# Own key tile of causal attention in fewer columns: values and probabilities repacked, the doubled high halves copied by VectorE

## The reference

```python
# x: (2, 512, 512) float32; Wq, Wo: 512 <-> 32*128; Wk, Wv: 512 -> 8*128
q = (x @ Wq).reshape(B, S, 32, 128).transpose(0, 2, 1, 3)
k = (x @ Wk).reshape(B, S,  8, 128).transpose(0, 2, 1, 3)   # each repeated for 4 query heads
v = (x @ Wv).reshape(B, S,  8, 128).transpose(0, 2, 1, 3)
scores = q @ k^T * 128 ** -0.5, masked causally
out = softmax(scores) @ v
x = layernorm(x + out.reshape(B, S, 4096) @ Wo)
# then a router with sparsemax over 8 low-rank experts:
base = x @ W_base^T + b_base
w = sparsemax(x @ W_router^T + b_router)
x = layernorm(x + base + sum_e w_e * (x @ A_e) @ B_e)
```

## Time and profile before

| | |
|---|---|
| median of 3 runs | 675.08 us (674.37 to 675.57) |
| span of the profiled execution | 673.6 us |
| TensorE busy | 657.9 us, 98%, 3605 matmuls |
| TensorE weight loads | 340.6 us, 51% |
| VectorE busy | 531.2 us, 79% |
| ScalarE busy | 416.8 us, 62% |
| GpSimd busy | 259.1 us, 38% |
| DMA moved | 71.80 MB, queue of SyncE and ScalarE 48.4% of 16 engines |

### The profile page before, as it was taken

How to read it: one execution, slowest core, us unless ns; L and a number is a source line. 1 busy time by engine, 2 the same in 40 slices (tenths; PEclk the granted TensorE clock), 3 DMA queues, 4 the chain that set the end, 5 groups by cost and what they waited for, 6 DMA issues and landing times.

```text
span 673.6 us, 11403 instructions
## 1 busy us (share of the span) xinstructions
PE 657.9 (98%) x3605; PEld 340.6 (51%) x3605; DVE 531.2 (79%) x1728; ACT 416.8 (62%) x1081; POOL 259.1 (38%) x246
## 2 busy tenths in 40 slices
PE   7899999999999999999999999999999999999996
PEld 3455455455555555455555545455554545455553
DVE  3899778867897688867797688867788578789866
ACT  3796665666556765667566765667556667866331
POOL 1686870166013750166013650167003613352231
PEclk9999999999999999999999999999999999999999
DMA  9357375354914285244924285353835247252602
GB/s 300 139 125 158 74 176 110 65 78 84 239 37 94 49 187 110 54 89 78 231 52 93 48 177 114 49 101 69 201 54 100 49 79 173 56 103 46 111 18 93
DMA packets 200779, 71.80 MB, mean 107 GB/s; under 512 B 169744, under 2 KB 192784, under 8 KB 200720
## 3 DMA queue, kind: packets, MB, share of 16 engines
q1 hardware_dynamic: 199376, 70.04, 48.4%
q10 hardware_dynamic: 1344, 1.05, 0.6%
HBM read 27.02 MB, written 2.10 MB: 43 GB/s over the span
## 4 chain that ended last, share of the span: by engine, by line
PE 89%; DVE 5%; DMA 3%; ACT 1%; POOL 1%; issue 1%; SPq 0%; DVEq 0%; POOLq 0%
PE bank L1259 23%; PE bank L1210 21%; PE bank L1249 15%; PE bank L1234 12%; PE bank L1222 5%; PE bank L1190 4%; PE bank L1291 2%; PE bank L1203 2%; PE bank L1193 2%; DMA pT<-p 2%; DVE p L1065 1%; PE bank L1183 1%; DVE pr L1045 1%; DVE rowmax L946 1%; PE bank L1302 1%
## 5 line engine op out<-in xcount | busy, mean ns | idle before, releaser
L741 POOL TENSOR_SCALAR raw<-raw,scale_of 128x512 f32<-128x512 f32 (+1 forms) x75 | 120.6, 1608 | 315.3 <-ACT wk L807 189.1
L1045 DVE CUSTOM_DVE_ANT_0 pr<-bank,mask,back_of 128x32 f32<-128x32 f32 (+15 forms) x256 | 125.3, 496 | 58.4 <-PE bank L1234 57.6
L863 ACT ACTIVATE pr<-pr,mx 128x288 f32<-128x288 f32 (+15 forms) x256 | 131.0, 512 | 61.2 <-DVE mx L1045 60.3
L1210 PE MATMUL bank<-xT,wq 128*128 128x512 f16 x720 | 164.5, 379 | 0.3 <-DVE y L1082 0.3
L872 ACT ACTIVATE p<-pr,ri 128x32 f16<-128x32 f32 (+15 forms) x256 | 118.4, 511 | 49.7 <-DVE ri L1056 49.5
L1065 DVE SCALAR_TENSOR_TENSOR p<-pr,ri,p 128x448 f16<-128x448 f32 (+15 forms) x256 | 128.4, 545 | 15.9 <-ACT p L872 14.7
L1234 PE MATMUL bank<-kT,qT 128*128 128x32 f16 (+15 forms) x768 | 122.2, 279 | 3.9 <-DVE qT L925 2.4
L1249 PE MATMUL bank<-pT,v 128*128 128x512 f16 x480 | 122.8, 379 | 0.8 <-DMA pT<-p 0.7
L1210 PEld LDWEIGHTS bank<-xT,wq 128*128 128x128 f16 x720 | 70.2, 98 | 82.1 <-DVE y L1082 0.8
L1234 PEld LDWEIGHTS bank<-kT,qT 128*128 128x128 f16 x768 | 67.7, 98 | 62.4 <-issue 3.9
L1259 PE MATMUL bank<-wo_odd,oT 128*128 128x512 f16 x384 | 96.1, 379 | 0.0
(11 more groups left out here) (145 smaller groups left out, 692.3 us busy)
## 6 DMA issues: line engine op xcount, KB each, us to landing
raw<-in_wo SPq DMA_DIRECT2D x32, 256.0 KB, 3.5
raw<-in_wq SPq DMA_DIRECT2D x30, 256.0 KB, 3.9
raw<-in_wk SPq DMA_DIRECT2D x8, 256.0 KB, 4.3
raw<-in_wv SPq DMA_DIRECT2D x8, 256.0 KB, 4.1
y<-in_x SPq DMA_DIRECT2D x1, 2048.0 KB, 13.0
pT<-p SPq DMA_TRANSPOSE x128, 3.7
out<-y SPq DMA_DIRECT2D x8, 256.0 KB, 2.0
pT<-in_xT SPq DMA_DIRECT2D x6, 256.0 KB, 7.7
```

The costliest lines, as they stand in the source:

```text
L741: eng.tensor_scalar(whole, raw_of(name, key), scale[0], None, ALU.mult).then_inc(sems["scaled"], 1)
L863: eng.activation(pr[:, t % 2, h, 0:w], pr[:, t % 2, h, 0:w], ACT.Exp, bias=mx[:, k:k + 1], scale=-1.0, accum_out=rs[:, k:k + 1]).then_inc( ...
L1045: eng.tensor_tensor_reduce(out=pr[:, t % 2, h, 0:w], in0=psum("S", t, h)[:, 0:w], in1=mask[:, 0:w], scale=score_scale(t), scalar=BIG, op0= ...
L1210: made = eng.matmul(out, wq[:, g % 2, w, h, c * 128:(c + 1) * 128], xT[:, x, c, b * 512:(b + 1) * 512], start=c == 0 and w + x == 0, stop= ...
```

## The change

The own key block (j = i) is multiplied differently. Of its 128 rows (keys) group 0 uses 32 and group 1 uses 64. In place of padding with zeros, the three products hi hi, hi lo and lo hi are laid side by side in the contraction: for group 0 three parts of 32 rows in one matmul of 128 columns, for group 1 two parts of 64 rows in one and its remaining product in another. For that the high half of the probabilities stands twice in p16, and the values need a second tile, vx, in which rows of v16 are copied to other partitions.

- TensorE: the own block takes six matmuls, of 256, 256, 128, 256, 128 and 128 columns, in place of three of 512. Before the first of them TensorE waits for all five copies of vx of this pair and batch row.
- SyncE: a new step VX(p, b, n), n = 0 to 4, copies a part of the values of pair p and batch row b into vx, after the low halves of its four blocks. `evicted` gives one VX behind each `rest` or `fetch` once the four `Vp_lo` have been given, and those still waiting right before the first step that reads them: the own PV, or the `rest` of the tile two further on.
- VectorE: for the first pair of groups of the tiles with i > 0, two copies double the high half (`tensor_copy`, 32 and 64 columns), and the subtraction of group 0 is done in two parts (32 columns and the others).
- ScalarE: for i = 0 it writes the high half of groups 0 and 1 twice by itself (a broadcast input).
- GpSimd: one memset of 32 partitions of vx at the start; the zeros in p16 are placed differently.
- The transpose of the first pair leaves out its first block of 128 columns, which nothing reads any more.
- The program reserves 1024 bytes a partition for descriptors of GpSimd's DMAs.

```diff
+VX_PARTS = 5
     if name == "PV":
         u = key[0] // NI
-        return [("Vp_lo", u // B // 2, 4 * (u % B) + key[1])]
+        packed = [("VX", u // B // 2, u % B, n) for n in range(VX_PARTS)] if key[1] == key[0] % NI else []
+        return [("Vp_lo", u // B // 2, 4 * (u % B) + key[1])] + packed
+    if name == "rest" and key[0] > 1:
+        u = (key[0] - 2) // NI
+        return [("VX", u // B // 2, u % B, n) for n in range(VX_PARTS)]
...
+    def packed(step):
+
+        if step[0] == "Vp_lo":
+            p, b = step[1], step[2] // 4
+            ready[p, b] = ready.get((p, b), 0) + 1
+            if ready[p, b] == 4:
+                waiting.extend(("VX", p, b, n) for n in range(VX_PARTS))
+
...
+        for x in [x for x in waiting if x in needed]:
+            waiting.remove(x)
+            yield x
         held = [x for x in held if x not in needed and x != (name, *key)]
         yield (name, *key)
+        packed((name, *key))
+        if name in ("rest", "fetch") and waiting:
+            yield waiting.pop(0)
...
+        vx = sb("vx", [128, 2, NV, 256], f16)
...
+            elif name == "VX":
+                count(f"vx{key[0]}{key[1]}", key[2], by=16)
...
+        def own_part(t, q, part):
+
+            w = 128 * (t % NI + 1)
+            at = 4 * w * (t % NI + q) + part * w
+            return p16[:, at:at + 128]
...
                     eng.dma_start_transpose(
-                        pT16[:, 2 * (t % 2) + q, 0:cols].rearrange("p (c n) -> p c n", n=128),
-                        probs(t, q)).then_inc(sems[f"turned{q}{t % 2}"], 16)
+                        pT16[:, 2 * (t % 2) + q, c0:4 * w].rearrange("p (c n) -> p c n", n=128),
+                        p16[:, at + c0:at + 4 * w]).then_inc(sems[f"turned{q}{t % 2}"], 16)
+                elif name == "VX":
+
+                    p, b, n = key
+                    s = v_slot(p, 4 * b)
+                    for tt in range(4 * b, 4 * b + 4):
+                        sp_.wait_ge(*done("v_lo", p, tt))
+                    to, part, of, at = ((0, 1, 1, 64), (64, 1, 0, 64), (32, 0, 0, 96), (64, 0, 1, 96), (96, 0, 0, 96))[n]
+                    eng.dma_start(vx[to:to + 128 - at, part, s:s + 4, :], v16[at:128, of, s:s + 4, :]).then_inc(sems[f"vx{p}{b}"], 16)
...
+                    eng.memset(vx[0:32, 0, :, :], 0.0).then_inc(sems["vx_zero"], 1)
...
-                        eng.activation(halves_of_probs(t, h)[0], pr[:, t % 2, h, 0:group(t, h)[1]], ACT.Copy,
+                        w, n = group(t, h)[1], 32 * (h + 1)
+                        if q == 0 and w == n:
+
+                            twice = pr[:, t % 2, h, 0:n].rearrange("p (a n) -> p a n", a=1).to_broadcast([128, 2, n])
+                            eng.activation(own_part(t, 0, h + 1)[:, 128 - 2 * n:128].rearrange("p (a n) -> p a n", a=2), twice, ACT.Copy,
+                                           scale=ri[:, 1, k:k + 1]).then_inc(sems["p_hi"], 1)
+                            continue
+                        eng.activation(halves_of_probs(t, h)[0], pr[:, t % 2, h, 0:w], ACT.Copy,
...
-                        made = eng.scalar_tensor_tensor(out=lo, in0=pr[:, t % 2, h, 0:group(t, h)[1]], scalar=ri[:, 1, k:k + 1], in1=hi,
-                                                        op0=ALU.mult, op1=ALU.subtract)
+                        w, n = group(t, h)[1], 0
+                        if h == 0:
+
+                            n = 32
+                            made = eng.scalar_tensor_tensor(out=own_part(t, 0, 1)[:, 32:64], in0=pr[:, t % 2, h, 0:n], scalar=ri[:, 1, k:k + 1],
+                                                            in1=hi[:, 0:n], op0=ALU.mult, op1=ALU.subtract)
+                        own = 32 * (h + 1)
+                        if q == 0 and own < w:
+
+                            made = eng.tensor_copy(own_part(t, 0, h + 1)[:, 128 - 2 * own:128 - own], hi[:, 0:own])
+                        if n < w:
+                            made = eng.scalar_tensor_tensor(out=lo[:, n:w], in0=pr[:, t % 2, h, n:w], scalar=ri[:, 1, k:k + 1], in1=hi[:, n:w],
+                                                            op0=ALU.mult, op1=ALU.subtract)
...
-                    for a, p in half3:
-                        made = eng.matmul(out, v16[:, a, s, cols], turned_of(t, j, p).rearrange('p a m (h n) -> p a m h n', n=32), start=j == 0 and a + p == 0,
-                                          stop=j == i and a == 1)
-                    if j == i:
-                        made.then_inc(sems["PV"], 1)
+                    turned = turned_of(t, j)
+                    hi, lo = turned[:, :, 1:3, :], turned[:, :, 0:4:3, :]
+                    vh, vl = v16[:, 0, s, cols], v16[:, 1, s, cols]
+                    if j < i:
+                        for v, p in ((vh, hi), (vh, lo), (vl, hi)):
+                            eng.matmul(out, v, p.rearrange("p a m (h n) -> p a m h n", n=32), start=j == 0 and v is vh and p is hi, stop=False)
+                    else:
+
+                        pe.wait_ge(*done(f"vx{g // 2}{b}", VX_PARTS - 1))
+                        pe.wait_ge(*done("vx_zero"))
+                        late = out[:, 1, :, :, :]
+                        eng.matmul(late, vh, hi[:, 1, :, :].rearrange("p m (h n) -> p m h n", n=32), start=j == 0, stop=False)
+                        eng.matmul(late, vh, lo[:, 1, :, :].rearrange("p m (h n) -> p m h n", n=32), start=False, stop=False)
+                        eng.matmul(out[:, 0, 1, :, :], vh, lo[:, 0, 1, :].rearrange("p (h n) -> p h n", n=32), start=False, stop=False)
+                        eng.matmul(late, vl, hi[:, 1, :, :].rearrange("p m (h n) -> p m h n", n=32), start=False, stop=False)
+                        eng.matmul(out[:, 0, 1, :, :], vx[:, 1, s, cols], hi[:, 0, 1, :].rearrange("p (h n) -> p h n", n=32), start=False, stop=False)
+                        eng.matmul(out[:, 0, 0, :, :], vx[:, 0, s, cols], hi[:, 0, 0, :].rearrange("p (h n) -> p h n", n=32), start=False,
+                                   stop=True).then_inc(sems["PV"], 1)
```

More of the change, by code:

```diff
@@ L34, in reads @@
         u = key[0] // NI
-        return [("Vp_lo", u // B // 2, 4 * (u % B) + key[1])]
+        packed = [("VX", u // B // 2, u % B, n) for n in range(VX_PARTS)] if key[1] == key[0] % NI else []
[3 more added lines that the diff above has]
+        return [("VX", u // B // 2, u % B, n) for n in range(VX_PARTS)]
     return [("O_lo", key[0])] if name == "W" else []
 def evicted(steps):
-    held, given = [], set()
+    held, given, ready, waiting = [], set(), {}, []
+    def packed(step):
[4 more added lines that the diff above has]
+                waiting.extend(("VX", p, b, n) for n in range(VX_PARTS))
     for name, *key in steps:
@@ L56, in evicted @@
                 yield x
+                packed(x)
             held = []
@@ L599, in group, with turned_of @@
             return 15 - (4 * (t % NI) + b), 32 * (4 * (t % NI) + b + 1)
[L601 to L605, removed]
+        def own_part(t, q, part):
+            w = 128 * (t % NI + 1)
+            at = 4 * w * (t % NI + q) + part * w
+            return p16[:, at:at + 128]
         def halves_of_probs(t, b):
-            both = probs(t, b // 2).rearrange("p (s m n) -> p s m n", s=2, m=2)
-            return [both[:, s, b % 2, 96 - 32 * b:] for s in range(2)]
-        def turned_of(t, j, s):
+            w = 128 * (t % NI + 1)
+            at = 4 * w * (t % NI + b // 2)
+            return [p16[:, at + part * w + 96 - 32 * b:at + (part + 1) * w] for part in ((1, 0) if b % 2 == 0 else (2, 3))]
+        def turned_of(t, j):
             w = 128 * (t % NI + 1)
             two = 2 * (t % 2)
-            x = pT16[:, two:two + 2, 0:4 * w].rearrange("p a (s h n) -> p a s h n", s=2, h=2)
             c = t % NI - j
-            return x[:, :, s, :, c * 128:(c + 1) * 128]
+            return pT16[:, two:two + 2, 0:4 * w].rearrange("p a (s n) -> p a s n", s=4)[:, :, :, c * 128:(c + 1) * 128]
         def most_pieces(kind, n, m=None):
@@ L678, in _ @@
                     t, q = key
-                    cols = 512 * (t % NI + 1)
+                    w = 128 * (t % NI + 1)
+                    at = 4 * w * (t % NI + q)
+                    c0 = 128 * (1 - q)
                     sp_.wait_ge(*done("zeros", t % NI, q))
@@ L754, in _ @@
                         pool.wait_ge(*done("squares", *of))
-                    both = probs(t, q).rearrange("p (s m n) -> p s m n", s=2, m=2)
-                    for m in range(2 - q):
-                        made = eng.memset(both[:, :, m, 0:96 - 32 * (2 * q + m)], 0.0)
+                    for part, n in ((0, 32), (1, 32)) if q else ((1, 32), (3, 64)):
+                        made = eng.memset(own_part(t, q, part)[:, 0:n], 0.0)
                     made.then_inc(sems["zeros"], 1)
@@ L1333 @@
     arrays = {n: np.ascontiguousarray(a) for n, a in arrays.items()}
-    nc = bacc.Bacc("TRN2", target_bir_lowering=False, num_devices=1)
```

(1 more changed line is left out.)

3 lines of the change are left out of this document (2 added, 1 removed).

## The result

The changed kernel takes 707.38 us (median of 4 runs, 704.89 to 708.28) against 675.17 for the kernel before: 1.0477 times as long, 95% interval 1.0455 to 1.0498. Slower was forecast, but 692 us, and the time lies above the range. The profiled execution is the fastest of the four, with a span of 703.1 us.

The account below looks back on a forecast made before the run. TensorE, busy back to back, bounds the kernel: span 673.6 - 9.8 (columns) + 20.5 and 1.5 (copy waits) + 2 (transposes) + 3 (clock) = 690.8 us; median 1.5 above, about 692; own range 685 to 699, whole range 680 to 703.

Parts of the forecast that it names:

- The columns: TensorE's own key tile: 1536 columns become 1152 in each of 64 tiles, a gain of 9.8 us.
- the rival by the weight loads: Short TensorE matmuls take a weight load's 94 ns, not 56, losing 7.3 us of the gain: 699; chance 0.03.
- The sign that I had named for a wrong column price: If TensorE's busy time doesn't fall (some 10 us less was expected), the price per column is wrong.
- SyncE's queue and the five waits: Fifth copy issued too late for PV(0,0), (4,0), (20,0), (36,0), (52,0): TensorE waits 2.5 to 5.3 us each.
- PV(16,0) and its like: PV(16,0), (32,0), (48,0): copies given some four tiles ahead, so hidden, without a wait.
- VectorE's lateness: VectorE's step 0.6 us longer a tile delays transposes: 0.6 us at three copy waits, 2 us over other places.
- The one us that I let be given back behind PV(0,0): PV(0,0)'s 2.5 us wait counted as 1.5, since TensorE's later wait for queries and its like go away.
- The clock: Some of four long TensorE waits end on the low clock: 3 us, between 0 and 10.7.
- Rival (2): The clock falls at every long wait and the copies' landings are slow: 704 us; chance 0.12.
- Late transposes: TensorE waits for transposes delayed by VectorE's longer steps: 2 us for all places, bounds 0 and 8.
- All go through SyncE's queue: Step SyncE: forty copies, 0.45 us each on its queue, one behind each rest or fetch, held against their first readers.
- My upper bound for it: Upper bound for late transposes from VectorE: 8 us, given as 48 tiles at a quarter of 0.6 us each.

Follow-up runs that it names:

- e1_all_at_once: Changed kernel with the five copies of a pair and batch row queued together right behind the fourth block's low half of values; 671.72 us.
- e3_copies_and_wait: Kernel before plus the copies in the changed places and TensorE's wait for them, old 512-column matmuls and VectorE step kept; 705.77 us.
- the twin on the same chip: Changed kernel with the five copies together, the very first five behind the fetch of wq(1,1), doublings still on VectorE; 671.67 us.
- e8_fill_whole: Changed kernel with 53 to 104 identity matmuls of 128 columns ahead of each of the five waits for copies; 703.88 us.
- e2_fill: Changed kernel with 72 identity matmuls of 128 columns ahead of the waits at PV(4,0), (20,0), (36,0) and (52,0), none at PV(0,0); 703.03 us.

## Why the prediction was wrong

*The columns*, 9.8 us: right. The columns' time fell by 9.7 us, 128 columns cost 56 ns in the own tile too, and the rival by the weight loads is out. The sign that I had named for a wrong column price, a busy time of TensorE that doesn't fall, came (657.9 and 657.2 us) and misled: the busy time holds the 7.8 us of slow matmuls. (192 pairs by 25 ns are 4.8 us, not 4.9.)

*SyncE's queue and the five waits*: the mechanism and all five places were right, and PV(16,0) and its like waited for nothing. The size was a little low: 2.5, 5.3, 5.0, 5.6 and 4.6 us forecast (with VectorE's lateness), 23.0 in all; measured 2.8, 5.6, 5.6, 5.7 and the remaining 4.3, 24.0. The landing was 2.8 us at PV(20,0) where I took 2.4, the issue 0.58 where I took 0.45. By the account, which also counts the way from the semaphore to the start, the copies are 24.8 us. The one us that I let be given back behind PV(0,0) came as 1.4: the kernel before has 0.5 and 0.9 us of waiting for queries at 57 and 59 us in its account, the changed one none.

*The clock*: the mechanism was named, but this term is one of the two that were mis-sized most: 3 us taken, 7.8 measured, within the bound of 10.7. I had read from the earlier trace rows that the clock falls some 4 us after the last matmul, and so let only some of four waits, of 4 to 5.5 us, bring it down. All four did, and it was low for 20.5 us in all. Rival (2), to which I gave 0.12, came nearest: its clock at every long wait is what happened, its slow landings are not. The Trainium skill (TensorE: Matmul & The Clock Gate, What's actually happening) has an idle engine put on half its clock until work brings it back, and the trace agrees at these four waits. By that page the clock falls at all four, which is another sum than mine; where the prediction says that the page gives no other sum, it is wrong. The three other executions took 1.8 to 3.4 us more than the profiled one, at mean clocks of 0.976 to 0.981 against 0.985. So the median probably carries more of this than the profiled execution did; it isn't shown, and the execution with the lowest clock is the shortest of the three.

*Late transposes*: 2 us taken, less the one given back; the other waits grew by 6.6. The step that failed is "All go through SyncE's queue": I held the forty transfers only against their own readers and not against what stands behind them in that queue. The first row's copies lie among the fetches ahead of rest(14,1), and the reader of that transpose pays for it with 1.6 to 2.3 us in each of three rounds, 5.8 us together. With the copies elsewhere and all else the same (`e1_all_at_once`) 0.95 us of the three is left. VectorE's lateness, to which I gave the whole 2 us, makes 1.7 us alone; its work was over-priced, 29 us forecast and 16.5 measured. (My upper bound for it was 48 x 0.15 = 7.2 us, not 8.) How the parts add is open. In the account VectorE's steps alone make 2.3 us of waits and the copies alone 3.9, together nearly the 6.6, though both come from executions longer than their medians. Against a plain sum stands `e3_copies_and_wait`: with the copies and the waits for them, but with neither VectorE's steps nor the fewer columns, it has 5.7 us of other waits against 6.3 in the kernel before, or 7.2 with the four waits that went with the low clock at 28 us.

So the sum of 690.8 us becomes 703.1 by 1.8 (copies, 24.8 for 23.0), 4.8 (clock), 5.6 (other waits, 6.6 for 2 - 1) and 0.1 (columns). The median lies another 4.3 us above that: 1.8 us between the span and the time of the same execution, and 2.5 us by which the profiled execution is shorter than the median.

## What to carry to other kernels

A kernel whose main engine never idles has room for fewer columns, but none for a transfer that is issued behind its first reader. Hold each new transfer against its reader's start in the trace, then hold everything behind it in the same queue too: here the place of forty small transfers was worth 36 us, nearly four times the 9.7 us that the change takes off the columns. When an added wait on TensorE is several microseconds long, put the low clock behind it into the sum: all eight waits for copies of 4.1 to 5.8 us, in the changed kernel and in `e3_copies_and_wait`, had it, for 1.4 to 2.6 us each. An operation moved from the engine in the chain to one with idle time can be worth trying: the doublings on ScalarE gave 2.5 us against the twin on the same chip.

## What the runs showed of the hardware

- A copy of 64 or 128 KB between partitions holds SyncE's queue 0.50 to 0.93 us and lands in 2.0 to 4.2 us, 2.3 in the median, which is less than the 3.5 us of a weight fetch of 256 KB.
- A copy of 32 or 64 half-precision columns takes VectorE 201 or 234 ns in the mean (line L1117 of the changed kernel, 48 each), but 168 and 175 ns in the median: single ones take up to 1.1 us. ScalarE does the same in 214 and 256 ns, and none takes over 257.
- The clock can fall sooner than the end of the kernel before suggested. At PV(20,0) TensorE ended at 245.9 and the clock was low from 249.0. In `e8_fill_whole` it was low even from 29.0 to 32.3, behind waits of 1.7, 0.4, 0.7 and 0.2 us in the 5 us ahead of it:

```profile
26.00:28.90 2.90, 1.77 (x21) 1.09 (x21) 2.34 (x13) 2.28 (x8) 2.73 (x3) 1.00 0.01 3
29.00:32.30 3.30, 3.30 (x16) 2.35 (x17) 3.26 (x8) 2.48 (x7) 2.75 (x4) 0.50 0.02 5
```

In the same stretch of the changed kernel, with the same waits, it stayed up; in `e2_fill` and `e3_copies_and_wait` it fell there as well. Waits of 2 to 3 us go both ways too: behind the wait of some 3 us at PV(0,0) it fell in these two kernels and stayed up in the changed one. What decides it is not settled by these runs.
